# Strassen's seven products for the projections of an attention block, over four heads, on one Trainium2 core

## The chip, the cores and the metric

The kernel runs on one core of one Trainium2 chip. The metric is device time in microseconds (us). Three timed runs of the kernel before gave 1202.74, 1202.82 and 1204.02 us, median 1202.82 us. All data are float32. The big matmuls are done as three single-pass matmuls on a split of each operand into a high part (`hi`, type fp32r) and a rest (`lo`): hi·hi + hi·lo + lo·hi. The helper `three` issues them, so lines L707 to L709 stand for nearly all of TensorE's work.

## The reference

Tokens: 2 batches of 512, hidden width 512. `xn = layernorm(x)`. Then

```
qkv  = silu(xn @ qkv_w.T)                  # 32 heads x (q, k, v) x 128
scan over blocks of 32 tokens per head:    # linear attention with per-head decay
    scores = (q k^T) * diag_decay;  out = scores v + (q*q_decay) kv
    kv     = kv*block_decay + (k*k_decay)^T v
attn = rmsnorm(all heads, over 4096) * norm_w
gate = sigmoid(xn @ gate_w.T)              # 4096 wide
y    = (gate * attn) @ out_w.T             # 4096 -> 512
ffn  = xn @ W_base.T + b + routed LoRA experts (top 2 of 8, rank 16)
out  = x + y + ffn
```

The projections (q, k, v, gate) are 1024 tokens x 512 x 16384 and are more than half of the arithmetic. The kernels replace the scan by the equal full form: for each head and batch, scores of 512 x 512 (lower blocks only), times a decay table, times v.

## The kernel before

`acc` holds x, later the sum of the output projection. The front normalises the tokens in two halves (batch 0 first), turns them with TensorE transposes and splits them into `xhi` and `xlo`. ScalarE meanwhile fills `decay`, the decay tables of all 32 heads (L355).

The main part is a loop over 16 groups of two heads; each group has four steps `s` (head `s // 2`, batch `s % 2`). A step on TensorE is: `project` q (4 slices of the hidden width x 3 matmuls of 128 x 512), `attend` of the step before, in the first two steps `project_v` (4 token tiles, 12 matmuls of 128 x 256 each), `project` k, `project` the gate, in two of the four steps `output` (4 tiles, 6 matmuls of 128 x 512 each), then `scores` of this step. Each engine has this order written out by hand in its own block; semaphores tie them. PSUM's eight banks are two for projections (`proj`), three for scores, one for `att`, two for output tiles (`outp`).

Around it: ScalarE reads a projection from PSUM into SBUF through Silu or Tanh (L409, L437, L447, L456), copies it to the `hi` part (L415, L441, L451), and splits weight chunks (L364). VectorE subtracts to get the `lo` part (L572, L580, L583), multiplies scores by the table (L597), splits them (L602), gates (L544, L549) and adds output tiles into `acc` (L555). GpSimd makes the `lo` part of the weights (L301, 128 x 512 each) and the sum of squares (L320). The SP queue loads weight chunks of 256 KB five slots ahead.

The tail (after the last group) does the router (L846), the last attention step, the top-2 routing as a chain of small VectorE operations (L640 to L678), the base and expert matmuls into all eight banks, and adds everything (L693, L697). The base matmul is 96 matmuls of 128 x 512.

Of the kernel before, what the change touches and what calls it, by code (L numbers as in the profile page):

```python
# [11 lines left out]
P = 128  # L26
# [5 lines left out]
GH = 2  # L32
GROUPS = HEADS // GH
STEPS = GH * BATCH
# [4 lines left out]

V_AT = (1, 1 + TB)  # L40
PROJ = 3 * STEPS + NTB
PROJ0 = (0, 3 + TB, 2 * (3 + TB), 2 * (3 + TB) + 3)


SPLIT = TB - 1
P_LEN = tuple(SEQ - P * j for j in range(TB))
P_AT = tuple(sum(P_LEN[:j]) for j in range(TB))
P_COLS = sum(P_LEN[:SPLIT])

ORDER = (3, 0, 1, 2)  # L50

FIRST_CHUNKS = 5
CONSTS = 5
RAW_SLOTS = 5
GROUP_CHUNKS = 10

# [9 lines left out]

def build(nc, x, w_chunks, norm_w, a_router, b_base, slopes, out):
    x_tok = x.rearrange("b (t p) c -> p (b t) c", p=P)  # L70
    out_tok = out.rearrange("b (t p) c -> p (b t) c", p=P)

    ctx = ExitStack()
    with ctx:
        def sb(name, shape, dt=F32):
            return ctx.enter_context(nc.sbuf_tensor(name, shape, dt))

        def bank(name):
            return ctx.enter_context(nc.psum_tensor(name, [P, 512], F32))
# [3 lines left out]


        xhi = sb("xhi", [P, KC, BATCH * SEQ], F32R)
        xlo = sb("xlo", [P, KC, BATCH * SEQ], F32R)

        acc = sb("acc", [P, NTB, HID])

        decay = sb("decay", [P, HEADS, 2 * P])  # L90
        table = sb("table", [P, SEQ])

        raw = sb("raw", [P, RAW_SLOTS, 512])
        qkg_hi = [sb(f"qkg_hi{i}", [P, 3, KC * P], F32R) for i in range(GH)]
        qkg_lo = [sb(f"qkg_lo{i}", [P, 3, KC * P], F32R) for i in range(GH)]
        wv_hi = sb("wv_hi", [P, 2, 512], F32R)
        wv_lo = sb("wv_lo", [P, 2, 512], F32R)
        wo_hi = sb("wo_hi", [P, GH, HID], F32R)
        wo_lo = sb("wo_lo", [P, GH, HID], F32R)

        qf = sb("qf", [P, SEQ])
        kf = sb("kf", [P, SEQ])
        q_hi = sb("q_hi", [P, SEQ], F32R)
        q_lo = sb("q_lo", [P, SEQ], F32R)
        k_hi = sb("k_hi", [P, SPLIT * P], F32R)
        k_lo = sb("k_lo", [P, SPLIT * P], F32R)
        vf = [sb(f"vf{i}", [P, GH * D]) for i in range(SPLIT)]
        v_hi = [sb(f"v_hi{b}", [P, SPLIT, GH * D], F32R) for b in range(BATCH)]
        v_lo = [sb(f"v_lo{b}", [P, SPLIT, GH * D], F32R) for b in range(BATCH)]
        v_last = [sb(f"v_last{b}", [P, GH * D]) for b in range(BATCH)]  # L110
        pf = sb("pf", [P, sum(P_LEN)])
        p_hi = sb("p_hi", [P, P_COLS], F32R)
        p_lo = sb("p_lo", [P, P_COLS], F32R)
        tanh_g = sb("tanh_g", [P, SEQ])
        square = sb("square", [P, SEQ])
        gated = sb("gated", [P, SEQ])
        g_hi = [sb(f"g_hi{s}", [P, SEQ], F32R) for s in range(STEPS)]
        g_lo = [sb(f"g_lo{s}", [P, SEQ], F32R) for s in range(STEPS)]
        sum_sq = sb("sum_sq", [P, BATCH, SEQ])

# [5 lines left out]
        half_norm = sb("half_norm", [P, HEADS])  # L126
        minus_half = sb("minus_half", [P, NTB])
# [5 lines left out]
        diff = square[:, 0:2 * P]  # L133

        free = decay[:, :, :].rearrange("p h n -> p (h n)")
        taken = [0]

        def take(*shape):
            n = 1
            for d in shape:  # L140
                n *= d
            part = free[:, taken[0]:taken[0] + n]
            taken[0] += n
            if len(shape) == 1:
                return part
            names = "abc"[:len(shape)]
            sizes = {k: d for k, d in zip(names, shape)}
            return part.rearrange(f"p ({' '.join(names)}) -> p {' '.join(names)}", **sizes)

        x_again = take(NTB, HID)  # L150
        ar = take(KC, ER + EXPERTS)
        base_b = take(HID)
        h_keep = take(NTB, ER)
        sm = [take(NTB, EXPERTS) for _ in range(8)]
        sm1 = [take(NTB) for _ in range(8)]
        xf = [qf, kf, pf[:, 0:HID], pf[:, HID:2 * HID]]
        hw_hi = g_hi[0:2]
        hw_lo = g_lo[0:2]

        proj = [bank(f"proj{i}") for i in range(2)]  # L160
        score = [bank(f"score{i}") for i in range(3)]
        att = bank("att")
        outp = [bank(f"outp{i}") for i in range(2)]
        S = {j: score[i % 3][:, 0:P_LEN[j]] for i, j in enumerate(ORDER)}

        turn = [score[0], score[1], att, outp[0]]
        ffn = [proj[0], proj[1], score[2], outp[0], outp[1], att, score[0], score[1]]


        x_in = [sem(f"x_in{t}") for t in range(NTB)]  # L170
        slope_in = sem("slope_in")
        raw_in = [sem(f"raw_in{i}") for i in range(RAW_SLOTS)]
        norm_in = sem("norm_in")
        again_in = sem("again_in")
        consts = sem("consts")
        diff_made = sem("diff_made")
        decay_made = sem("decay_made")
        ln = sem("ln")
        pow_ready = sem("pow_ready")
        pow_done = sem("pow_done")  # L180
        xn_ready = sem("xn_ready")
        turned = sem("turned")
        xhi_done = sem("xhi_done")
        xlo_done = sem("xlo_done")
        acc_zero = sem("acc_zero")
        whi_done = sem("whi_done")
        wlo_done = sem("wlo_done")
        proj_ready = sem("proj_ready")
        proj_free = sem("proj_free")
        qhi_done = sem("qhi_done")  # L190
        qlo_done = sem("qlo_done")
        khi_done = sem("khi_done")
        klo_done = sem("klo_done")
        vhi_done = sem("vhi_done")
        vlo_done = sem("vlo_done")
        gate_done = sem("gate_done")
        table_done = sem("table_done")
        scores_ready = sem("scores_ready")
        masked = sem("masked")
        phi_done = sem("phi_done")  # L200
        plo_done = sem("plo_done")
        att_ready = sem("att_ready")
        gated_done = sem("gated_done")
        ghi_done = sem("ghi_done")
        glo_done = sem("glo_done")
        square_done = sem("square_done")
        summed = sem("summed")
        out_ready = sem("out_ready")
        acc_done = sem("acc_done")
        late_in = sem("late_in")  # L210
        xf_done = sem("xf_done")
        h_ready = sem("h_ready")
        h_read = sem("h_read")
        route = sem("route")
        route_act = sem("route_act")
        rms_ready = sem("rms_ready")
        hw_done = sem("hw_done")
        hw_turned = sem("hw_turned")
        hwhi_done = sem("hwhi_done")
        hwlo_done = sem("hwlo_done")  # L220
        xb_done = sem("xb_done")
        part_done = sem("part_done")
        ffn_ready = sem("ffn_ready")
        result_done = sem("result_done")
        stored = sem("stored")

# [694 lines left out]
```

## Time and profile before

| quantity | value |
|---|---|
| time, median of three | 1202.82 us |
| profiled execution: span | 1201.3 us |
| profiled execution: its own time | not given apart from the span; the median lies 1.5 us above the span |
| TensorE (PE) busy | 1170.9 us, 97% of the span |
| VectorE (DVE) busy | 716.2 us, 60% |
| ScalarE (ACT) busy | 523.2 us, 44% |
| GpSimd (POOL) busy | 343.4 us, 29% |
| granted TensorE clock | 1.000 of full speed |

PE's busy time counts matmuls that overlap in the pipeline, so a row's duration (0.39 us for 128 x 512) is longer than the step from one matmul to the next; that step is the useful price, and is read as the distance between start times. PEld is the weight load, which runs beside the matmuls. For the other engines, a duration includes an end that overlaps the next instruction of the same engine when that one waits for nothing.

### The profile page before, as it was taken

The numbers are of one execution on the slowest core, as the hardware profiler recorded it, in microseconds if no ns is written. First come the engines' busy times: TensorE is split into PE (matmuls) and PEld (weight loads), VectorE is DVE, ScalarE is ACT, GpSimd is POOL, SyncE is SP. The second block draws the span as 40 slices with busy tenths as digits, with TensorE's granted clock in tenths as the row PEclk, the third lists the DMA queues.
The fourth block names the chain that finished last, engine by engine and source line by source line (L and its number), as shares of the span: only waits on it lengthen the run. The fifth ranks groups of instructions, "written<-read, shape, count | busy, mean of one in ns | idle before, by whom it ended". The sixth has DMA issues, their size and how long they took to land.

```text
span 1201.3 us, 18952 instructions
## 1 busy us (share of the span) xinstructions
PE 1170.9 (97%) x6256; PEld 1013.1 (84%) x6256; DVE 716.2 (60%) x1216; ACT 523.2 (44%) x1076; POOL 343.4 (29%) x253
## 2 busy tenths in 40 slices
PE   5999999999999999999999999999999999999998
PEld 4888888888888888888888888888888888888887
DVE  6664655656565664655556465655656556465667
ACT  7543535434453543445344343543445354344520
POOL 3332313313231331323223131331323133132323
PEclk9999999999999999999999999999999999999999
DMA  4121101101011110201101010110111111020301
GB/s 159 36 53 36 53 18 44 44 17 52 27 43 35 33 54 18 52 17 44 44 22 54 29 52 17 44 44 17 52 35 40 30 36 51 17 52 25 106 1 70
DMA packets 27694, 50.31 MB, mean 42 GB/s; under 512 B 3232, under 2 KB 3232, under 8 KB 27680
## 3 DMA queue, kind: packets, MB, share of 16 engines
q1 hardware_dynamic: 27392, 50.10, 14.2%
q8 instruction: 8, 0.13, 0.0%
q10 hardware_dynamic: 288, 0.03, 0.0%
q14 instruction: 6, 0.05, 0.0%
HBM read 48.02 MB, written 2.10 MB: 42 GB/s over the span
## 4 chain that ended last, share of the span: by engine, by line
PE 83%; ACT 6%; DVE 5%; issue 5%; DMA 0%; ACTq 0%; POOL 0%; DVEq 0%; SPq 0%; POOLq 0%
PE proj L707 17%; PE proj L709 16%; PE proj L708 16%; PE outp L707 5%; PE outp L709 5%; PE outp L708 5%; PE score L709 3%; PE score L708 3%; PE score L707 3%; PE att L707 2%; PE att L709 2%; PE att L708 2%; DVE k_lo L583 2%; DVE gated L544 2%; PE score L779 2%
## 5 line engine op out<-in xcount | busy, mean ns | idle before, releaser
L707 PE MATMUL proj<-xhi,qkg_hi 128*128 128x512 f32 x768 | 303.5, 395 | 1.5 <-DVE xlo L525 1.5
L709 PE MATMUL proj<-xhi,qkg_lo 128*128 128x512 f32 x768 | 299.7, 390 | 0.0
L708 PE MATMUL proj<-xlo,qkg_hi 128*128 128x512 f32 x768 | 299.7, 390 | 0.0
L301 POOL TENSOR_TENSOR qkg_lo<-raw,qkg_hi 128x512 fp32r<-128x512 f32 x99 | 128.0, 1294 | 565.6 <-ACT qkg_hi L364 565.6
L462 ACT ACTIVATE p_hi<-pf 128x512 fp32r<-128x512 f32 (+2 forms) x192 | 86.6, 515 | 247.0 <-DVE pf L597 247.0
L709 PEld LDWEIGHTS proj<-xhi,qkg_lo 128*128 128x128 f32 x768 | 144.1, 188 | 31.5
L707 PEld LDWEIGHTS proj<-xhi,qkg_hi 128*128 128x128 f32 x768 | 144.4, 188 | 27.7 <-DVE xlo L525 1.8
L708 PEld LDWEIGHTS proj<-xlo,qkg_hi 128*128 128x128 f32 x768 | 144.5, 188 | 26.0
L555 DVE TENSOR_TENSOR acc<-acc,outp 128x512 f32<-128x512 f32 x128 | 88.1, 688 | 116.0 <-PE outp L709 116.0
L707 PE MATMUL proj<-wv_hi,xhi 128*128 128x256 f32 (+1 forms) x514 | 151.0, 294 | 4.1 <-ACT vf L437 2.6
L572 DVE TENSOR_TENSOR q_lo<-qf,q_hi 128x512 fp32r<-128x512 f32 x64 | 86.7, 1354 | 112.7 <-ACT q_hi L415 112.7
L709 PE MATMUL proj<-wv_hi,xlo 128*128 128x256 f32 (+1 forms) x514 | 145.4, 283 | 0.0
L708 PE MATMUL proj<-wv_lo,xhi 128*128 128x256 f32 (+1 forms) x514 | 145.4, 283 | 0.0
L597 DVE TENSOR_TENSOR pf<-score,table 128x128 f32<-128x128 f32 (+3 forms) x256 | 113.7, 486 | 43.4 <-PE score L779 33.9
L549 DVE TENSOR_TENSOR g_lo<-gated,g_hi 128x512 fp32r<-128x512 f32 x64 | 104.7, 1636 | 46.0 <-ACT g_hi L427 45.3
L583 DVE TENSOR_TENSOR k_lo<-kf,k_hi 128x384 fp32r<-128x384 f32 x64 | 65.9, 1029 | 90.3 <-ACT k_hi L451 88.2
L320 POOL TENSOR_TENSOR sum_sq<-sum_sq,square 128x512 f32<-128x512 f32 x64 | 109.0, 1704 | 24.1 <-ACT square L471 22.7
L707 PEld LDWEIGHTS proj<-wv_hi,xhi 128*128 128x128 f32 x514 | 98.1, 191 | 10.5 <-ACT vf L437 10.4
L301 POOL TENSOR_TENSOR wo_lo<-raw,wo_hi 128x512 fp32r<-128x512 f32 x32 | 41.2, 1286 | 219.8 <-ACT wo_hi L364 219.8
L707 PE MATMUL outp<-wo_hi,g_hi 128*128 128x512 f32 x256 | 99.7, 389 | 1.1 <-DVE g_lo L549 1.1
L708 PE MATMUL outp<-wo_lo,g_hi 128*128 128x512 f32 x256 | 99.6, 389 | 0.0
L709 PE MATMUL outp<-wo_hi,g_lo 128*128 128x512 f32 x256 | 99.6, 389 | 0.0
(193 smaller groups left out, 1978.2 us busy)
## 6 DMA issues: line engine op xcount, KB each, us to landing
raw<-w_chunks SPq DMA_DIRECT2D x165, 256.0 KB, 2.6
acc<-x SPq DMA_DIRECT2D x8, 256.0 KB, 5.9
decay<-x SPq DMA_DIRECT2D x1, 2048.0 KB, 10.6
out<-acc SPq DMA_DIRECT2D x8, 256.0 KB, 2.0
decay<-a_router SPq DMA_DIRECT2D x1, 272.0 KB, 3.0
decay<-b_base SPq DMA_DIRECT2D x1, 256.0 KB, 5.1
slope<-slopes ACTq DMA_DIRECT2D x1, 16.0 KB, 5.0
norm<-norm_w ACTq DMA_DIRECT2D x1, 16.0 KB, 5.5
```

The source lines that it names most:

```text
L301: pool.tensor_tensor(lo, raw[:, slot, :], hi.bitcast(F32), ALU.subtract).then_inc(wlo_done, 1)
L320: pool.tensor_tensor(sum_sq[:, b, :], sum_sq[:, b, :], square[:], ALU.add).then_inc(summed, 1)
L462: act.activation(p_hi[:, cols], pf[:, cols], ACT.Copy).then_inc(phi_done, 1)
L544: dve.tensor_tensor(gated[:], att[:, :], tanh_g[:], ALU.mult).then_inc(gated_done, 1)
L549: dve.tensor_tensor(g_lo[s][:], gated[:], g_hi[s][:].bitcast(F32), ALU.subtract).then_inc(glo_done, 1)
L555: dve.tensor_tensor(acc[:, b * TB + t, :], acc[:, b * TB + t, :], outp[t % 2][:, :], ALU.add).then_inc(acc_done, 1)
L572: dve.tensor_tensor(q_lo[:], qf[:], q_hi[:].bitcast(F32), ALU.subtract).then_inc(qlo_done, 1)
L583: dve.tensor_tensor(k_lo[:], kf[:, 0:SPLIT * P], k_hi[:].bitcast(F32), ALU.subtract).then_inc(klo_done, 1)
L597: dve.tensor_tensor(pf[:, P_AT[j]:P_AT[j] + P_LEN[j]], S[j], table[:, 0:P_LEN[j]], ALU.mult).then_inc(masked, 1)
L707: pe.matmul(out_, a_hi, b_hi, start=start, stop=False)
L708: pe.matmul(out_, a_hi, b_lo, start=False, stop=False)
L709: return pe.matmul(out_, a_lo, b_hi, start=False, stop=stop)
```

## The change

All of `build` is rewritten. What it does:

**Products.** Tokens of the two batches and the two halves of the hidden width form a 2 x 2 block matrix (t). Two heads' columns (or two heads' q and k) form the other (w). A *unit* computes all four blocks of the product, 128 x 512 each times two, by seven products instead of eight (Strassen in Winograd's form). A product is 2 slices x 3 = 6 matmuls of 128 x 512, or 12 of 128 x 256 where tokens are the stationary side (units V1, V2 and the base matmul). The seven token operands `t_hi`, `t_lo` are made once in the front. The weight operands are made for each unit: GpSimd makes four combinations of 128 x 256 (`combine`), ScalarE copies seven blocks of 256 to `w_hi` (`weight`), GpSimd subtracts for `w_lo` (`low`).

**Putting the products together** takes three PSUM banks p, q, r and one SBUF tile x (`xs`): per unit ScalarE copies three results to SBUF (`copy_m1`, `copy_u2`, `copy_u3`) and VectorE adds three times (`make_u2`, `make_c22`, `make_c12`), each 128 x 512. TensorE may start product 7 only after `copy_u2`, product 4 after `copy_u3`, product 3 after `make_c22`. Products 1, 6 and 5 open the banks p, q and r anew and wait until the unit before has been drained from them (`free`).

**Loops.** The main loop has 8 bodies (first, 6 in a hardware loop, last) of four heads: units V1, V2 (v of four heads), QK1, QK2, QK3 and QK0 (q and k of a head, QK0 for the next body), G23, G01 (gates). In the last body QK0 and G01 are the base matmul. Two units (QK0, G01 of the first body) come ahead of the loop.

**Operands stay in PSUM.** Silu is applied in place in the bank; the table is multiplied in place in the score bank; gating is done in place in `att`. So the `lo` subtractions read one operand from PSUM, except for the tile x. `outp` has one bank instead of two.

**Front and tail.** The router and the top-2 routing move to the front, with the eight tiles normalised together; the decay tables go to DRAM (`near_dram`, 4 MB written) and come back one head at a time; the x + bias term goes through DRAM too. The tail keeps four output tiles, the expert matmuls and the sums.

Core of the diff, TensorE's side:

```diff
+            def product(g, i, m, by_token=False):
+                n = unit(g, i)
+                b = BANK_OF[m]
+                if m in (1, 5, 6):
+                    at_least(pe, free[b], n)
+                else:
+                    pe.wait_ge({7: u2_copied, 2: m1_copied, 4: u3_copied, 3: c22_made}[m], n + 1)
...
+                pe.wait_ge(wlo[PIECE_OF[m]], n + (2 if by_token and pair == 0 else 1))
...
+                    for kc in range(2):
+                        w = slice(kc * P, kc * P + P)
+                        mm = three(banks[b], w_hi[i % 2][:, wi, w], w_lo[i % 2][:, wi, w], t_hi[:, ti, kc, :], t_lo[:, ti, kc, :],
+                                   fresh and kc == 0, kc == 1)
...
+                output(-4)
+                scores(0)
+                output(-3)
+                prod(V1, 1, 6)
+                output(-2)
+                prod(V1, 5, 7, 2, 4, 3)
+                prod(V2, 1, 6)
+                output(-1)
+                prod(V2, 5, 7, 2, 4, 3)
+                attend(0)
+                scores(1)
+                prod(QK1, 1, 6, 5, 7, 2)
+                attend(1)
+                prod(QK1, 4, 3)
+                prod(QK2, 1, 6, 5)
+                scores(2)
+                prod(QK2, 7, 2, 4, 3)
+                attend(2)
+                scores(3)
+                prod(G23, 1, 6)
+                output(0)
+                prod(G23, 5)
+                output(1)
...
+                prod(G01, 2)
+                output(11)
+                attend(7)
+                prod(G01, 4, 3)
```

VectorE's and ScalarE's orders at four places (VectorE after V1 and after QK1, ScalarE in QK1 and at the end of a body):

```diff
+                make_c22(V1)
+                lo(V1, "p")
+                make_c12(V1)
+                lo(V1, "x")
+                lo(V1, "q")
+                lo(V1, "r")
+                make_u2(V2)
...
+                make_c12(QK1)
+                lo(QK1, "q")
+                gated_lo(1)
+                make_u2(QK2)
+                lo(QK1, "r")
...
+                probs01(1)
+                copy_m1(QK1)
+                gated_hi(0)
+                probs2(1)
+                out_weight(0)
+                copy_u2(QK1)
...
+                gate(G01, "p")
+                squares(7)
+                gate(G01, "q")
+                gated_hi(7)
```

The front on VectorE (`routing` is the chain of small operations) and on ScalarE:

```diff
+            make_u2(LAST + G01)
+            make_far(0)
+            make_c22(LAST + G01)
+            make_c12(LAST + G01)
+            routing()
+            dve.wait_ge(near_made, HEADS + 2)
...
+            weight(V1, 1)
+            weight(V1, 2)
+            silu(LAST + QK0, "p")
```

## Rows read from the trace of the kernel before

**Rows 1.** The page's first part: busy time of each engine, share, instructions.

```profile
PE 1170.9 (97%) x6256; PEld 1013.1 (84%) x6256; DVE 716.2 (60%) x1216; ACT 523.2 (44%) x1076; POOL 343.4 (29%) x253
```

**Rows 2.** TensorE's waits: engine and line that waited, for whom, us in total, times, longest.

```profile
PE score L716 <- DVE acc L519: 13.2, 1, 13.2
```

**Rows 3.** Three stretches (front, one group, tail): length, busy and instructions per engine, clock.

```profile
0.00:18.00 18.00, 3.29 (x16) 3.08 (x16) 9.84 (x22) 12.51 (x33) 5.49 (x15) 1.00 0.58 206
...
520.00:591.20 71.20, 70.49 (x378) 61.02 (x378) 41.72 (x69) 31.34 (x64) 19.84 (x14) 1.00 0.12 37
...
1156.00:1201.30 45.30, 40.97 (x224) 34.82 (x222) 31.94 (x88) 3.97 (x6) 13.35 (x10) 0.99 0.13 47
```

**Rows 4.** Timeline, TensorE: start us, duration us, line, operation; pairs that give a distance.

```profile
500.20 0.39 PE L707 MATMUL proj<-xhi,qkg_hi 128*128 128x512 f32 x1
...
500.88 0.39 PE L707 MATMUL proj<-xhi,qkg_hi 128*128 128x512 f32 x1
...
509.04 0.38 PE L779 MATMUL score<-qf,kf 128*128 128x128 f32 x2
...
510.85 0.39 PE L707 MATMUL proj<-xhi,qkg_hi 128*128 128x512 f32 x1
...
513.61 0.39 PE L707 MATMUL att<-p_hi,v_hi 128*128 128x512 f32 x1
...
515.33 0.36 PE L707 MATMUL proj<-wv_hi,xhi 128*128 128x256 f32 x1
...
515.76 0.28 PE L707 MATMUL proj<-wv_hi,xhi 128*128 128x256 f32 x1
...
516.12 0.28 PE L707 MATMUL proj<-wv_hi,xhi 128*128 128x256 f32 x1
```

**Rows 5.** Timeline, VectorE's table of a group's first head, in groups 1 and 7.

```profile
86.54 0.48 DVE L568 TENSOR_SCALAR table<-decay,far 128x128 f32 x2
...
513.57 0.48 DVE L568 TENSOR_SCALAR table<-decay,far 128x128 f32 x2
```

**Rows 6.** Groups by line and shape: busy us, mean ns, idle before.

```profile
L555 DVE TENSOR_TENSOR acc<-acc,outp 128x512 f32<-128x512 f32 x128 | 88.1, 688 | 116.0 <-PE outp L709 116.0
...
L572 DVE TENSOR_TENSOR q_lo<-qf,q_hi 128x512 fp32r<-128x512 f32 x64 | 86.7, 1354 | 112.7 <-ACT q_hi L415 112.7
...
L409 ACT ACTIVATE qf<-proj 128x512 f32<-128x512 f32 x64 | 38.3, 599 | 103.0 <-PE proj L709 103.0
...
L364 ACT ACTIVATE qkg_hi<-raw 128x512 fp32r<-128x512 f32 x98 | 60.9, 623 | 0.0
...
L301 POOL TENSOR_TENSOR qkg_lo<-raw,qkg_hi 128x512 fp32r<-128x512 f32 x99 | 128.0, 1294 | 565.6 <-ACT qkg_hi L364 565.6
```

**Rows 7.** Timeline of handovers: who starts how long after whom.

```profile
499.04 1.74 POOL L320 TENSOR_TENSOR sum_sq<-sum_sq,square 128x512 f32<-128x512 f32 x1
...
499.55 0.68 DVE L544 TENSOR_TENSOR gated<-att,tanh_g 128x512 f32<-128x512 f32 x1
...
500.65 0.39 PE L709 MATMUL proj<-xhi,qkg_lo 128*128 128x512 f32 x1
...
501.08 0.60 ACT L447 ACTIVATE kf<-proj 128x512 f32<-128x512 f32 x1 [0.18 <-PE proj L709]
...
1111.37 0.39 PE L707 MATMUL proj<-wv_hi,xhi 128*128 128x256 f32 x1 [0.18 <-ACT vf L437]
```

**Rows 8.** Timeline: runs on ScalarE and VectorE, part of the routing chain, the last sum.

```profile
2.96 8.07 ACT L355 ACTIVATE decay<-square 128x256 f32<-128x256 f32 x26
...
17.88 2.46 DVE L505 BATCH_NORM_STATS2 stats<-acc 128x6 f32<-128x512 f32 x4
...
1176.51 0.21 DVE L658 TENSOR_REDUCE decay<-decay 128x8 f32<-128x64 f32 x1
...
1182.32 1.71 DVE L678 TENSOR_TENSOR decay<-decay 128x128 f32<-128x128 f32 x8
...
1198.15 0.69 DVE L693 TENSOR_TENSOR acc<-score,acc 128x512 f32<-128x512 f32 x1 [1.77 <-PE score L709]
```

More of the change, by code:

```diff
@@ L150, in build @@
[L150 to L163, printed above, removed]
@@ new lines, in _ @@
+            whole(LAST + QK0, "p")
+            silu(LAST + QK0, "q")
+            hi(LAST + QK0, "p")
+            whole(LAST + QK0, "q")
+            weight(V1, 4)
+            hi(LAST + QK0, "q")
+            silu(LAST + QK0, "r")
+            weight(V1, 3)
+            whole(LAST + QK0, "r")
+            whole(LAST + QK0, "x")
+            hi(LAST + QK0, "r")
+            hi(LAST + QK0, "x")
+            weight(V2, 1)
+            copy_m1(LAST + G01)
+            copy_u2(LAST + G01)
+            copy_u3(LAST + G01)
@@ L477, in _ @@
+            weight(V2, 2)
+            gate(LAST + G01, "p")
+            gate(LAST + G01, "q")
+            gate(LAST + G01, "x")
+            weight(V2, 3)
             for t in range(2):
                 act.wait_ge(hw_turned, t + 1)
-                act.activation(hw_hi[t][:], score[t][:, :], ACT.Copy).then_inc(hwhi_done, 1)
+                copy(hw_t[:, 512 * t:512 * t + 512], score[:, t, :]).then_inc(hwt_done, 1)
+            act.wait_ge(near_out, 64)
+            body(0, first=True)
+            with act.Fori(1, SGS - 1) as g:
+                body(g)
@@ new lines, in _ @@
+            make_u2, make_c22, make_c12, lo = units(0)
+            for t in range(NTB):
+                dve.wait_ge(x_in[t], 16)
+                dve.bn_stats(stats[:, t, :], acc[:, t, :]).then_inc(ln, 1)
+            done[0] += NTB
+            dve.wait_ge(ln, done[0])
+            for t in range(NTB):
+                dve.bn_aggr(mean_var[:, t, :], stats[:, t, :]).then_inc(ln, 1)
+            done[0] += NTB
+            dve.wait_ge(ln, done[0])
+            dve.tensor_scalar(rs[:, 0, :], mean_var[:, :, 1], EPS, None, ALU.add).then_inc(pow_ready, 1)
@@ L869, in _ @@
-            base(5)
-            pe.wait_ge(hwlo_done, 2)
-            for t in range(NTB):
-                if t >= 6:
-                    base(t)
-                expert(t)
+            pe.wait_ge(hwt_done, 2)
+            body(0, first=True)
+            with pe.Fori(1, SGS - 1) as g:
+                body(g)
+            body(SGS - 1, final=True)
 def kernel(L0_attn_hidden_states, L0_attn_qkv_w, L0_attn_out_w, L0_attn_gate_w, L0_attn_norm_w,
```

1769 lines of the change are left out of this document (1173 added, 596 removed).

## The prediction

> **What bounds the kernel now.** I read the busy shares first: TensorE has work in 97% of the span, no other engine more than 60% [rows 1]. Next, its waits: the only long one is the 13.2 us before its first transpose [rows 2]. Then the stretches: a front of 18.0 us in which TensorE does 3.3 us, groups in which it is busy 70.5 of 71.2 us, a tail of 45.3 us; the granted clock is 1.00 to 0.99, its upper level of 2.4 GHz, throughout [rows 3]. So TensorE's own steps set the time, and a change is worth what it takes off them plus what it does to the front, the tail and the waits.
>
> The timeline gives the steps. Three matmuls of 128x512 take 500.88 - 500.20 = 0.68 us, 0.2275 each; three of 128x256 take 0.36 us, 0.120 each; one `scores` takes 510.85 - 509.04 = 1.81 us, one `attend` 515.33 - 513.61 = 1.72 us [rows 4]. A group has 144 projection matmuls (32.8 us), 96 of 256 for v (11.5), 48 for output tiles (10.9) and 4 x 3.53 (14.1): 69.3 us. The group's real period is (513.57 - 86.54)/6 = 71.17 us [rows 5], so 1.9 us of a group are waits. Four heads cost 142.3 us now.
>
> **TensorE's steps after the change.** A unit has 7 x 6 = 42 matmuls of 512 instead of 48: 9.56 us; by token 84 of 256, 10.1 us. A body: six units 57.3, two by token 20.2, 16 output tiles x 6 x 0.2275 = 21.8, eight scores and attends 28.2: 127.5 us, against 138.6 for two groups' steps. The first body lacks four output tiles (-5.5), the last has two units by token (+1.1). Eight bodies: 1020 - 5.5 + 1.1 = 1015.6 us.
>
> **Do the other engines have room?** Prices: VectorE 0.69 us for 128x512 with a PSUM operand, ScalarE 0.60 to 0.62, GpSimd 1.29 [rows 6]; 26 ScalarE instructions of 256 in a row take 8.07 us, 0.31 each [rows 8], from which 512 in a row is about 0.52 and each has 0.1 fixed. ScalarE in a body: 166 instructions over 73,700 columns (24 product copies, 44 Silu and whole parts, 24 high parts, 34 weight copies and so on); at 0.83 ns a column and 0.1 each, 61 + 17 = 78 us. VectorE: 137 instructions over 59,400 columns, at 1.05 ns and 0.15 each 62 + 21 = 83 us. GpSimd: 74 instructions over 28,700 columns; at 1.29/512 a column 72 us, with sums of squares at 1.74 [rows 7] 76 us. Its combinations of 256 columns have no row: half of 1.29 at least, 1.29 at most, by which the 76 could be 107; I take the lower, as the bulk is columns. An instruction that also writes PSUM in place has no row either; the nearest reads PSUM at 0.69, and I take that; from 0.1 less to 0.2 more for some 60 of them moves VectorE to 77 to 95 us. All stay below 127.5, so none is a bound by its sum. What remains is where TensorE waits for a short chain.
>
> The `lo` subtractions change in kind. `q_lo`, with two SBUF operands, takes 1.35 us [rows 6], while `gated`, which reads PSUM, took 0.68 inside a GpSimd instruction (499.04 to 500.78) [rows 7]. After the change all but those of tile x read PSUM; I price them at 0.69 and tile x at 0.69 to 1.35.
>
> **Waits inside a body.** Handover prices: the consumer starts 0.03 to 0.04 us after the producer's row ends (500.65 + 0.39, then 501.08; I take the same between the others), a matmul's row ends 0.16 after the next could start (0.39 - 0.2275), so a reader starts 0.2 us after TensorE has gone on; a restart costs 0.1 (0.39 against 0.28 at 1111.37) [rows 7]. A product is 1.365 us.
>
> - Product 7 needs product 6, `make_u2`, `copy_u2`: 0.2 + 0.69 + 0.03 + 0.60 + 0.04 = 1.56 us, with product 5 (1.365) above it. In seven units an output tile or `scores` stands between as well. In QK1 nothing does, and ScalarE has `gated_hi(0)`, `probs2(1)` and `out_weight(0)` (1024 columns, 0.95) ahead of `copy_u2`, whose chunk is asked for only when QK1's weights are split. I work out 0.5 to 1.6; I take 0.8 us.
> - V1 to V2: product 6 of V2 needs bank q drained. ScalarE is done with q in time, but VectorE's order has `make_c12` (product 3's end + 0.2 + 0.69), then `lo` of x (0.69 to 1.35), then `lo` of q (0.69). From product 3's end this is 2.3 to 2.9 us, against 1.44 for product 1 of V2: 0.9 to 1.5; I take 1.2.
> - QK1 to QK2: `lo(QK1,"q")` ends 1.5 us after product 3, against 1.365: 0.25 with the restart. Then the real one: VectorE does `make_u2(QK2)` before `lo(QK1,"r")`. So product 5 of QK2, which opens r, waits for product 6's end + 0.2 + 0.69, then 0.56 for 384 columns, + 0.1: 1.55 us.
> - End of a body: `output(-4)` needs attend(7)'s squares, gating, `gated_hi`, `gated_lo`: 0.8, 1.5, then ScalarE first does `gate(G01,"q")`, which waits for product 4 (to 2.2), then 2.8, 3.5 us, against 2.73 for products 4 and 3: 0.9 with the restart.
> - Products 4 and 3 have 0.5 and 1.2 us to spare over `copy_u3` and `make_c22`; QK3 and QK0 have an attend ahead of the next unit; weights come 2 us or more ahead. I take nothing for them.
>
> Sum 4.8 us a body, 38 in all. Bodies: 1054 us, a period of 132.3 against 142.3.
>
> **The front grows.** Eight tiles are normalised together: four tiles' statistics take 2.46 us [rows 8], so eight, the last load among them, end near 11 us (an estimate); with power, refinement and eight tiles through TensorE and ScalarE (0.52 each, beside two splits) they are turned by 22. Token operands are nine passes of 1024 columns on VectorE (1.2 each), two SBUF operands each, beside three of 2.6 on GpSimd; by the `q_lo` row a meeting costs 0.66; a pass that meets one of these might wait 2.6. I allow 3 us in all, from 1 to 8. Product 1 starts near 20, but products 5, 6, 7, 4 wait one by one for their operands; the first unit ends at 38. ScalarE meanwhile does twelve tables (12 x 0.31), a table load, then G01's weights; it then stands in `weight(V1,2)` until GpSimd has made G01's lower parts (4.6) and V1's combinations (3), to 50, before it drains the first unit's banks. So G01 runs from 53 to 64. `routing()` stands behind `make_c12` on VectorE: from L658 on it takes 1182.32 + 1.71 - 1176.51 = 7.5 us [rows 8], some 2 more before that. With two copies the first `scores` starts at 76 us; from 64 on nothing hides the 12 us. Now the first projection starts at 18.0 [rows 3]. 76, from 68 to 86.
>
> The Trainium skill, "SBUF — State Buffer", section "Who interferes with whom", says that a VectorE instruction with two SBUF inputs and a GpSimd instruction that reads SBUF exclude each other, the later one blocked until the other's end. By it three meetings would cost up to 7.8 us instead of the 3, the front would be 81 and the sum 1163; the `q_lo` and `gated` rows agree with it.
>
> **The tail shrinks.** After the last product VectorE does `make_c12` and base sums (0.69 each, to 3.7), two experts, refinement (6.4), then four output tiles through one bank: each 1.365 + 0.2 + 0.69, to 14.0; six expert sums, eight results (0.66 each) and a refinement, 24.4; the last store lies 1201.3 - 1198.84 = 2.5 us behind the last sum [rows 3, 8]: 27 us, from 24 to 31, where now the stretch is 45.3, which holds the base matmul.
>
> **Sum.** 76 + 1054 + 27 = 1157 us of span; the median lies 1.5 above the span of the profiled execution: 1158.5. Against 1201.3: front +58, groups 1139 to 1054, tail -18.
>
> **Rivals.**
> - *Waits small.* If the orders interlock better than my worst readings (2 us a body, not 4.8) and the front is 70: 1130 us. For it: the present orders leave only 1.9 us a group [rows 5]. Against it: the `make_u2` before `lo` of r is in the code. 0.15.
> - *ScalarE late at the copies (the other side).* ScalarE works in order, and each unit needs it at `copy_u2` and `copy_u3` within 0.5 us. If at seven units a body a weight copy (0.3 to 0.95 us) that waits for GpSimd or a chunk stands in front, each costs about 1.2 us beyond my sum, 8.4 a body: 1158 + 67 = 1225 us. It decides from 5.6 us a body beyond the 4.8, where 1203 is reached. For it: GpSimd's 76 us may be 107, and it holds ScalarE at every second and fourth weight piece. Against: weights stand two units ahead, and sums leave 40% free. 0.12.
> - *Half of that*, 1170 to 1203: 2 to 5 us a body more than I found. 0.23.
> - *The clock falls.* In short stops between matmuls, or in the 12 us stop, the granted clock could go to 1.2 GHz, where steps double; 5% of the bodies at that level would cost 50 us: 1208. The row of the front shows 1.00 with TensorE idle for 15 of 18 us [rows 3]. The Trainium skill, "TensorE: Matmul & The Clock Gate", section "A second HAM failure mode: psum-queue depth-cycling", says small idle times between groups of matmuls can make the clock go up and down; the trace of before does not show it. 0.03.
> - *It does not save the products.* The count of matmuls in the code is plain: below 0.01.
>
> **How the numbers follow.** My forecast's case (1138 to 1175) has 0.47, predicted 1158. The range of 8 in 10 takes the small-waits case and nearly all of the half case: 1125 to 1203. Below 0.2% (2.4 us) a measurement of this kernel can't tell a change from none. Slower than 1205: the late copies, part of the clock case: 0.12. Within: 0.02. Faster: 0.86.
>
> **What would show it.** TensorE's count near 5,900 instead of 6256, in steps of 0.2275 us; a body period of 132 us; the longest repeated wait at product 5 of QK2 for `lo` of r, then product 6 of V2, the tile at the body's start and product 7 of QK1; the first `scores` at 76 us after a stop of some 12; tail 27 us; `lo` at 0.69 us from PSUM. I am wrong if the period is above 138, if GpSimd's busy share is above 80%, or if TensorE waits at `copy_u2` or `copy_u3` in most units.

## The result: slower, with the profile after

The changed kernel takes 1243.2 us (median of 4 runs, 1241.9 to 1244.1) against 1202.8: a ratio of 1.033, 95% interval 1.032 to 1.034. Forecast were 1158.5 us, 1125 to 1203. The profiled execution has a span of 1241.8 us, 1.4 below the median. Two of the kernels below had one run each far outside all others (3259 and 2571 us), which their medians and ranges leave out.

First the page of the kernel after: busy times as in [rows 1], then the span in 40 slices, TensorE's busy tenths and its granted clock.

```profile
PE 1118.3 (90%) x5848; PEld 956.0 (77%) x5848; DVE 689.5 (56%) x1212; ACT 679.7 (55%) x1401; POOL 641.2 (52%) x629
...
PE   3477989989999899989999899989999899989995
...
PEclk9779899999999899989999899989999899989999
```

The reader is to see two things. TensorE has 408 matmuls fewer, as it should, and is busy 90% of the span, no longer 97%. Single slices, again and again, show 8 instead of 9, in the busy row and in the clock row alike: something in each body stops TensorE, and behind it the clock is lower.

TensorE's waits, as in [rows 2]: for whom, us in total, times, longest.

```profile
PE bank_q L1350 <- ACT ys L531: 40.0, 9, 7.1
PE score L1528 <- DVE acc L1260: 20.3, 1, 20.3
PE bank_p L1350 <- DVE q_lo L979: 14.2, 1, 14.2
PE bank_r L1350 <- DVE q_lo L979: 11.0, 8, 1.4
PE score L1552 <- DVE h_keep L1327: 6.7, 1, 6.7
PE outp L1350 <- DVE g_lo L1052: 5.9, 7, 0.9
...
PE bank_q L1350 <- DVE v_lo L979: 4.4, 8, 0.5
```

The four waits that the forecast had named are the four that repeat in the bodies, and three are its size or smaller. `ys` is what `copy_u2` writes: the wait of product 7 of QK1, forecast at 0.8 us, is eight of the nine waits and 35.2 of the 40.0; it is 3.8 to 4.4 us in bodies 2 to 8 and 7.1 in the first, which has the ninth, of 4.8, too.

The stretches, with columns as in [rows 3]: the front up to the first `scores`, the loop's bodies from 240 to 1080, one body from product 6 of V2 to the same in the next, 8.2 us of that body, and the tail.

```profile
0.00:85.15 85.15, 39.58 (x189) 32.77 (x189) 44.27 (x88) 43.54 (x94) 43.45 (x46) 0.85 0.35 120
...
240.00:1080.00 840.00, 798.52 (x4161) 682.73 (x4160) 470.95 (x823) 483.79 (x997) 447.64 (x444) 0.98 0.13 41
...
529.99:669.80 139.81, 133.00 (x692) 113.68 (x693) 78.35 (x137) 80.54 (x168) 74.62 (x74) 0.98 0.13 41
551.80:560.00 8.20, 8.11 (x27) 6.65 (x28) 1.38 (x3) 4.26 (x11) 5.71 (x4) 0.66 0.24 78
...
1213.40:1241.80 28.40, 15.30 (x66) 11.08 (x64) 18.09 (x36) 0.00 (x0) 2.49 (x2) 0.91 0.20 74
```

Against the forecast's span of 1157:

| part | forecast us | measured us |
|---|---|---|
| front, to the first `scores` | 76 | 85.15 |
| eight bodies | 1054 | 1128.25 |
| of them a steady body's period | 132.3 | 139.8 |
| tail | 27 | 28.4 |
| span | 1157 | 1241.8 |

Of the 84.8 us missing, 74 lie in the bodies: 7.5 for each of eight, and 14 more: some 13 in the first body, the rest in the last.

Now one of these stops in the timeline (start, duration, engine, line, and in brackets how long the engine was idle before and whom it waited for).

```profile
542.28 1.29 POOL L391 TENSOR_TENSOR w_lo<-raw,w_hi 128x512 fp32r<-128x512 f32 x1 [3.05 <-ACT w_hi L531]
...
545.69 0.28 DVE L1027 TENSOR_TENSOR p_end<-score,table 128x128 f32<-128x128 f32 x1
...
546.30 0.33 SPq L263 DMA_DIRECT2D table<-near_dram  x1
...
546.90 0.86 SPq L249 DMA_DIRECT2D raw<-w_chunks  x2
...
550.29 1.06 ACT L531 ACTIVATE wo_hi<-raw 128x1024 fp32r<-128x1024 f32 x1 [3.56 <-DMA raw<-w_chunks]
...
551.26 0.58 ACT L531 ACTIVATE ys<-bank_q 128x512 f32<-128x512 f32 x1
...
551.89 0.79 PE L1350 MATMUL bank_q<-t_hi,w_hi 128*128 128x512 f32 x1 [3.93 <-ACT ys L531]
...
552.48 0.63 PE L1351 MATMUL bank_q<-t_lo,w_hi 128*128 128x512 f32 x1
```

Read from the end. Product 7 waits 3.93 us for `copy_u2` (`ys`). `copy_u2` stands behind `out_weight(0)` (`wo_hi`), for whose chunk ScalarE was idle 3.56 us. GpSimd had done with that chunk's buffer at 543.57. But SyncE issued the load only at 546.90: ahead of it in its queue is `load_near(4 * g + 1)`, the next head's tables, which waits until VectorE has used the tables that stand in its place (L1027, 545.69). So 3.3 us passed in SyncE's queue. And the matmuls behind the stop last 0.79 and 0.63 us in steps of 0.43, where 0.39 and 0.2275 are usual: the granted clock is 0.66 in the mean of the 8.2 us, so in most of them it is 0.5, the lower level of 1.2 GHz.

Against a body without this stop (first experiment below) the period is 5.6 us longer. The stop has 3.1 of them (3.93 against 0.86). The other 2.5 are what is left, and the slow matmuls make up nearly all of it: 12 matmuls in steps of 0.43 in place of 0.2275 are 2.4 us.

### The profile page after: what moved, and what is told of

Its sections match the earlier page's. It is cut to its first block, busy times and chain, and to the rows that moved or that the text cites. A ratio compares the mean times of both kernels' runs of the same rounds, so it can differ in the third digit from the quotient of the medians.

```text
span 1241.8 us, 18953 instructions
## 1 busy us (share of the span) xinstructions
PE 1118.3 (90%) x5848; PEld 956.0 (77%) x5848; DVE 689.5 (56%) x1212; ACT 679.7 (55%) x1401; POOL 641.2 (52%) x629
## 4 chain that ended last, share of the span: by engine, by line
PE 78%; DVE 9%; issue 4%; DMA 3%; ACT 3%; POOL 1%; SPq 1%; DVEq 0%; ACTq 0%; POOLq 0%
PE bank_q L1350 8%; PE bank_q L1352 7%; PE bank_q L1351 7%; PE outp L1350 5%; PE outp L1352 4%; PE outp L1351 4%; PE bank_p L1351 4%; PE bank_p L1350 4%; PE bank_p L1352 4%; PE bank_r L1350 4%; PE bank_r L1352 4%; PE bank_r L1351 4%; PE att L1350 3%; PE att L1352 3%; PE att L1351 3%
## 5 line engine op out<-in xcount | busy, mean ns | idle before, releaser
L391 POOL TENSOR_TENSOR w_lo<-combo,w_hi 128x768 fp32r<-128x768 f32 (+1 forms) x132 | 170.1, 1291 | 206.5 <-ACT w_hi L531 206.2
L391 POOL TENSOR_TENSOR w_lo<-raw,w_hi 128x256 fp32r<-128x256 f32 (+1 forms) x132 | 135.6, 1032 | 172.0 <-ACT w_hi L531 171.8
L1350 PE MATMUL bank_q<-t_hi,w_hi 128*128 128x512 f32 x288 | 121.9, 423 | 43.7 <-ACT ys L531 40.0
L1352 PE MATMUL bank_q<-t_hi,w_lo 128*128 128x512 f32 x288 | 118.1, 410 | 0.0
L1351 PE MATMUL bank_q<-t_lo,w_hi 128*128 128x512 f32 x288 | 117.8, 409 | 0.0
L531 ACT ACTIVATE p_hi<-score 128x896 fp32r<-128x896 f32 (+1 forms) x128 | 81.2, 653 | 62.5 <-DVE score L1020 62.3
L1350 PE MATMUL outp<-wo_hi,g_hi 128*128 128x512 f32 x256 | 103.0, 403 | 12.2 <-DVE g_lo L1052 5.9
L1350 PEld LDWEIGHTS bank_q<-t_hi,w_hi 128*128 128x128 f32 x288 | 56.6, 197 | 61.6 <-ACT ys L531 43.8
L1350 PE MATMUL bank_p<-t_hi,w_hi 128*128 128x512 f32 x192 | 79.9, 416 | 14.2 <-DVE q_lo L979 14.2
L1350 PE MATMUL bank_r<-t_hi,w_hi 128*128 128x512 f32 x192 | 76.1, 396 | 11.0 <-DVE q_lo L979 11.0
L531 ACT ACTIVATE w_hi<-combo 128x768 fp32r<-128x768 f32 (+1 forms) x132 | 81.2, 628 | 8.7 <-POOL combo L384 6.8
L1351 PE MATMUL bank_p<-t_lo,w_hi 128*128 128x512 f32 x192 | 79.6, 415 | 0.0
L1352 PE MATMUL bank_p<-t_hi,w_lo 128*128 128x512 f32 x192 | 79.3, 413 | 0.0
```

The costliest lines, as they stand in the source:

```text
L391: pool.tensor_tensor(piece(w_lo[i % 2], j), piece_source(i, j), piece(w_hi[i % 2], j).bitcast(F32), ALU.subtract).then_inc(wlo[j], 1)
L531: return act.activation(out_, in_, ACT.Copy, **kw)
L1350: pe.matmul(out_, a_hi, b_hi, start=start, stop=False, skip_group_check=True)
L1351: pe.matmul(out_, a_hi, b_lo, start=False, stop=False, skip_group_check=True)
L1352: return pe.matmul(out_, a_lo, b_hi, start=False, stop=stop, skip_group_check=True)
```

## The experiments

Theory after the comparison: (A) the late chunk in SyncE's queue delays `copy_u2`, and the stop brings the lower clock with it. Rivals: (B) ScalarE's order alone, whatever the chunk; (C) the clock falls by the kernel's many short stops, not by this one. All times are medians, ratios are to the kernel before, run on the same chip.

**SyncE's order alone.** In a body the chunk for `out_weight(0)` is asked for ahead of the tables:

```diff
-                load_near(4 * g + 1)
                 unit_taken(g, QK1)
                 load_rows(0, 20 * g + 8, 20 * g + 9)
+                load_near(4 * g + 1)
```

> SP's order: the load of the output weights' chunk (asked for when QK1's weights are split) goes ahead of the load of the decay table of head 1, which waits in the same queue until step 1's scores are masked. ScalarE's order unchanged. Theory A': the chunk is late because of that wait in SP's queue: it is issued 3.2 us earlier (right after GpSimd's 543.57 instead of 546.90), product 7's wait falls from 3.9 to about 1.0 us, the clock stays up, 1197 us. Theory D (the chunk is late because of its transfer, or GpSimd): no change, 1240 or more.

Measured: 1203.4 us (1200.8 to 1209.7, 10 runs), ratio 1.0006 (0.9991 to 1.0021): 39.8 us less than the changed kernel. Its timeline around product 7, then the six bodies from 240 to 1080:

```profile
532.38 0.94 SPq L249 DMA_DIRECT2D raw<-w_chunks  x2
534.79 0.33 SPq L263 DMA_DIRECT2D table<-near_dram  x1
...
535.84 1.06 ACT L531 ACTIVATE wo_hi<-raw 128x1024 fp32r<-128x1024 f32 x1 [0.49 <-DMA raw<-w_chunks]
...
536.80 0.58 ACT L531 ACTIVATE ys<-bank_q 128x512 f32<-128x512 f32 x1
...
537.43 0.50 PE L1350 MATMUL bank_q<-t_hi,w_hi 128*128 128x512 f32 x1 [0.86 <-ACT ys L531]
...
240.00:1080.00 840.00, 817.18 (x4378) 702.29 (x4377) 504.08 (x854) 505.95 (x1045) 464.41 (x458) 1.00 0.13 42
```

The load now goes 2.4 us ahead of the tables, `ys` is in time, product 7 waits 0.86 us (0.43 to 0.94 over bodies 2 to 8), which is the 0.8 of the forecast, and the loop's clock is 1.00. The period is 134.2 us. The time is 6 us above the expected 1197: the first body takes 147.0 us where it took 147.3, since stops of 3.60, 2.35, 3.31 and 4.78 us stand there in place of 7.10 and 4.79. (C) falls here: with stops of 0.43 to 1.38 us in every body the clock does not move. The forecast had cited a rule beside its clock rival (the Trainium skill, "TensorE: Matmul & The Clock Gate", section "A second HAM failure mode: psum-queue depth-cycling": small idle times between groups of matmuls can make the clock go up and down): for these stops the trace does not agree. One exchange of two lines in a queue that does no arithmetic was worth nearly half of the miss.

**ScalarE's order alone.** `copy_u2(QK1)` and `copy_u3(QK1)` ahead of `out_weight(0)` and two weight pieces; SyncE as in the changed kernel:

```diff
-                out_weight(0)
                 copy_u2(QK1)
+                copy_u3(QK1)
+                out_weight(0)
                 weight(QK2, 2)
                 weight(QK2, 4)
-                copy_u3(QK1)
```

> ScalarE's order in QK1: copy_u2 and copy_u3 ahead of out_weight(0) and QK2's weight copies. Theory A (product 7 of QK1 waits only because copy_u2 stands in ScalarE's queue behind out_weight(0), whose chunk lands late, and the stop lets the clock fall to its lower level, which costs 2.6 us more a body): the 3.9 us wait goes to 0.4, the granted clock stays 1.00 from the second body on, the period falls from 139.8 to about 133.7, the time from 1243 to about 1191 us. Theory B (the low clock comes from the body's load, not from the stop): the wait goes but the stretches at half clock stay, about 1215 us. Theory C (the wait only moves, to QK2's weights): above 1230 us.

Measured: 1232.5 us (1230.6 to 1234.6), 1.0245 (1.0228 to 1.0263). Product 7's wait in QK1 is gone, and another grew: `PE bank_r L1350 <- DVE q_lo L979`, product 5 of QK2, 23.2 us in 8 waits where it had been 11.0. Of a body's 139.8 us only 1.7 were won. The time is that of the third theory, though the wait moved to another place than it said. (B), ScalarE's order alone, does not explain the loss.

**Both together**, the two edits above in one kernel.

> Both edits (copies first, chunk first). Theory A and A': product 7's wait 0.3 to 0.4, nothing behind it late, clock 1.00 in the loop: 133.5 us a body, about 1188 us; at most 4 us better than copies first alone. If GpSimd's lower parts were the next to be late, the chunk's earlier load would help more, 1180.

Measured: 1232.0 us (1229.6 to 1234.0), 1.0238 (1.0219 to 1.0256), no better than ScalarE's order alone and 29 us worse than SyncE's. A miss, and the most useful one. Its timeline, then its six bodies:

```profile
408.75 0.60 ACT L531 ACTIVATE xs<-bank_q 128x512 f32<-128x512 f32 x1 [1.75 <-PE bank_q L1352]
409.24 1.05 ACT L531 ACTIVATE wo_hi<-raw 128x1024 fp32r<-128x1024 f32 x1
...
416.31 8.69 SPq L249 DMA_DIRECT2D raw<-w_chunks  x5
...
419.61 0.42 ACT L531 ACTIVATE w_hi<-raw 128x256 fp32r<-128x256 f32 x1 [2.12 <-DMA raw<-w_chunks]
...
419.93 0.58 ACT L531 ACTIVATE q_hi<-bank_r 128x512 fp32r<-128x512 f32 x1
...
421.29 0.52 PE L1350 MATMUL bank_r<-t_hi,w_hi 128*128 128x512 f32 x1 [2.90 <-DVE q_lo L979]
...
422.03 0.63 PE L1352 MATMUL bank_r<-t_hi,w_lo 128*128 128x512 f32 x1
...
240.00:1080.00 840.00, 807.07 (x4243) 691.62 (x4242) 479.81 (x830) 489.58 (x1009) 448.46 (x444) 0.98 0.13 41
```

`out_weight(0)` (`wo_hi`) came later on ScalarE, now behind `copy_u3` (`xs`), which waits for product 7 itself. So its lower part came later on GpSimd, so the buffer came free later and the next chunks were loaded later; ScalarE then stood 2.12 us in `weight(G23, 1)`, which is ahead of `hi(QK1, "r")` in its order. A copy moved forward had put a wait for a transfer in front of another copy. (That `copy_u3` is the one is shown below, by the kernel that moves `copy_u2` alone.) The lower clock came back too (0.63 us matmuls, 0.98).

**Keep the stop, by another cause.** `copy_u2` first as above, but TensorE waits for `out_weight(0)` before product 7 of QK1:

```diff
-                prod(QK1, 1, 6, 5, 7, 2)
+                prod(QK1, 1, 6, 5)
+                pe.wait_ge(wohi, 2 * g + 1)
+                prod(QK1, 7, 2)
```

> copy_u2 ahead of out_weight(0) on ScalarE, but TensorE itself waits, before product 7 of QK1, until out_weight(0) is done: the same stop of about 3.8 us, held by a wait of TensorE's own. Theory A: the stop alone makes both losses, so the time stays at 1240 to 1246 us with the same half-clock stretch of 6.8 us in each body. Theory B or any in which ScalarE's lateness has other victims: clearly below, 1215 to 1230 us.

Measured: 1233.7 us (1232.0 to 1238.2), 1.0243 (1.0222 to 1.0263), period 139.0, 31.4 us in 8 waits there. This lies between the two expectations. Against the kernel with SyncE's order mended, the stop alone keeps 4.8 of the 5.6 us a body, with ScalarE free to run on; it is also a little shorter, and shrinks from 3.83 us in body 2 to 3.20 in body 8. These are the 8 us behind it in bodies 4, 5 and 8, after stops of 3.64, 3.40 and 3.20 us:

```profile
552.00:560.00 8.00, 8.00 (x26) 6.53 (x27) 1.27 (x2) 4.06 (x10) 6.08 (x4) 0.62 0.18 46
691.60:699.60 8.00, 8.00 (x32) 6.72 (x33) 2.35 (x4) 4.71 (x11) 6.85 (x5) 0.81 0.15 47
1106.01:1114.01 8.00, 8.00 (x38) 6.79 (x39) 3.35 (x5) 6.03 (x14) 7.73 (x5) 1.00 0.19 52
```

The granted clock is 0.62, 0.81 and 1.00: in this place the longer stop has more slow matmuls behind it, and that of 3.20 us has none.

**A stop of another length**, on the kernel with SyncE's order mended: TensorE waits for VectorE's second table before product 7.

```diff
+                pe.wait_ge(tab_made, 8 * g + 4)
```

> Base: chunk first (1203.4 us). Added: TensorE waits before product 7 of QK1 until VectorE has made head 1's far tables, a stop of some 1.5 to 2.5 us in each body where it was 0.65, and nothing else is held. Theory A (a stop of 3.9 us brings the clock down, a short one does not): the granted clock stays 1.00 in the loop, the time grows by the longer stop alone, 1 to 2 us a body: 1211 to 1219 us. Theory B (any added stop costs clock as well): half-clock stretches in the loop, 1230 us or more.

Measured: 1218.5 us (1216.5 to 1219.5), 1.013 (1.011 to 1.015), period 136.5, at the upper end of the first theory. Its product 7 and its six bodies:

```profile
404.48 0.50 PE L1350 MATMUL bank_q<-t_hi,w_hi 128*128 128x512 f32 x1 [3.13 <-DVE table L986]
...
240.00:1080.00 840.00, 803.44 (x4307) 690.67 (x4307) 491.86 (x839) 496.77 (x1027) 453.11 (x449) 1.00 0.13 41
```

The stop of 3.13 us costs 2.3 us a body more than the one of 0.7 in the mean that it replaces, and nothing else: the clock stays at 1.00. So stops are paid at least once, and the changed kernel's 3.93 us stop, and the 2.90 us one above, are paid a second time in slow matmuls. At product 7 of QK1, in bodies 2 to 8, the cases part by length: no slow matmul behind the eight stops of 3.12 to 3.20 us in this kernel and the one that keeps the stop; in that one 6 to 8 behind those of 3.31 to 3.46; and 7 to 13 behind those of 3.59 to 4.36, there and in the changed kernel. Across places they do not: at product 5 of QK2, in the two kernels with both copies first, all stops of 2.77 to 3.08 us have 6 to 13 slow matmuls behind them; TensorE had worked only 1.7 us between each and another stop of 0.7 to 1.0. And with SyncE's order alone, a stop of 3.60 us in the first body has none. What decides besides the length, these runs do not settle.

**The waits that the forecast had named.** Two more kernels, on top of SyncE's order. One puts `copy_u2(QK1)` ahead of `out_weight(0)` only, `copy_u3` where it was:

```diff
-                out_weight(0)
                 copy_u2(QK1)
+                out_weight(0)
```

> Base: chunk first. Added: only copy_u2(QK1) ahead of out_weight(0); copy_u3 keeps its place behind the weight copies. The wait of product 7 falls from 0.65 to 0.2 us, product 5 of QK2 unchanged: 1199 to 1201 us. If any delay of out_weight(0) makes GpSimd late and G23's chunk with it (what both edits together showed), product 5 of QK2 waits longer and the time is 1208 or more.

Measured: 1199.7 us (1198.2 to 1201.3), 0.9966 (0.9953 to 0.9978), period 133.7, as expected. This kernel differs from the one of both edits (1232.0 us) only in the place of `copy_u3`: `wo_hi` starts 0.15 us ahead of product 7 here and 2.19 us behind it there, and the wait of product 5 of QK2 is 1.38 us here and 2.90 there. So it was `copy_u3` that must not stand ahead of `out_weight(0)`.

The other lets bank r be drained first, on both engines:

```diff
+                lo(QK1, "r")
                 make_u2(QK2)
-                lo(QK1, "r")
...
-                copy_m1(QK2)
                 whole(QK1, "r")
-                weight(G23, 1)
                 hi(QK1, "r")
+                copy_m1(QK2)
+                weight(G23, 1)
```

> Base: chunk first. Added: VectorE makes the lower part of r (QK1) ahead of make_u2(QK2), and ScalarE makes its high part ahead of copy_m1(QK2) and G23's first weight copy. The forecast's third term: product 5 of QK2 waits 1.38 us now and 0.1 then, 1.3 us a body: 1193 us. If make_u2, now later, holds product 7 of QK2 instead: 1200 or more.

Measured: 1195.0 us (1191.0 to 1195.4), 0.992 (0.990 to 0.994), period 132.9. The wait of product 5 of QK2 is gone from the list: 1.3 us a body for the stop that the forecast had at 1.55.

**All orders together**: the three above, `lo` of q before `lo` of x behind V1, `gated_hi(7)` before `gate(G01, "q")`, in the front the first unit's copies ahead of V1's weights, and `weight(QK0, 1)` behind `copy_u2(G23)`. The last of these, as an example:

```diff
-                weight(QK0, 1)
                 copy_m1(G23)
                 copy_u2(G23)
+                weight(QK0, 1)
```

> Chunk first, u2 first, lo r first, and three more: lo of q ahead of lo of x after V1; gated_hi(7) ahead of the gate of q; in the front, the first unit's Silu and high parts ahead of V1's weight copies; QK0's first weight copy behind copy_u2(G23). Per body 0.4 + 1.3 + 0.5 + 0.8 = 3.0 us off 134.0; front 6 us earlier; first body's stop of 4.8 us gone: 1203 - 24 - 6 - 5 = 1168 us. If GpSimd's chain is the next bound, above 1180.

Measured: 1177.5 us (1175.3 to 1180.1), 0.978 (0.976 to 0.980), period 131.4; the first `scores` comes at 79.3. That is 9.5 us above the expected 1168, though the period fell by 2.8 us of the expected 3.0 and the front by 5.7 of 6. What is left of stops in a body is 0.29 and 0.42 us. The first body still had three, of 3.60, 4.65 and 1.90 us.

**The routing earlier.** On top of it:

```diff
             make_c12(LAST + G01)
-            routing()
...
+            routing()
             lo(LAST + QK0, "p")
```

> All the reorderings of the run with everything together, and `routing()` moved on VectorE from behind the gates' combinations to ahead of `lo` of the front's first unit, where VectorE is idle. Theory (the front is set by the order in which the routing, the tables and the first `scores` follow one another): the first `scores` comes at 72 to 74 us in the place of 79.3, the rest of the kernel stays, and the time is near 1171 us. Rival (the front is set by the passes over the tokens, whose lengths grow where GpSimd and VectorE meet; the routing is hidden): the first `scores` stays at 79 and the time at 1177.5 us, or worse where the routing now stands in front of the first unit's `lo`.

Measured: 1177.9 us (1177.3 to 1179.5), 0.979 (0.978 to 0.981): nothing. The theory fell. TensorE's two marks in the front are

```profile
65.97 0.79 PE L1350 MATMUL bank_p<-t_hi,w_hi 128*128 128x512 f32 x1 [18.43 <-DVE q_lo L979]
...
80.07 0.50 PE L1350 MATMUL score<-q_hi,k_hi 128*128 128x512 f32 x1 [0.74 <-ACT acc L531]
```

against 56.87 and 79.30 before the move. The stop of 7.11 us at the router's transposes is gone, and the one at bank p has grown from 8.09 to 18.43: VectorE does the routing from 49 to 65, and `lo` of the first unit, which frees bank p, stands behind it. The chain of small operations is the bound in either place, and it is not the same length in both. In its old place it took 7.8 us (70.2 to 78.0), in the new one 16.0 (49.35 to 65.3), while GpSimd makes the lower parts and combinations of the weights. Its last eight multiplications, after the move and before it:

```profile
59.46 5.85 DVE L1327 TENSOR_TENSOR h_keep<-h_keep,sm 128x128 f32<-128x128 f32 x8
...
76.30 1.70 DVE L1327 TENSOR_TENSOR h_keep<-h_keep,sm 128x128 f32<-128x128 f32 x8
```

The move was expected to gain 5 to 7 us, and the chain is 8.2 us longer beside GpSimd's work, which is enough to undo it. No run tested this by itself.

**The bias trip out of the first body.** On top of this one, tokens plus bias go through the DRAM earlier: GpSimd's first addition in the front, the second behind `combine(QK1)`, SyncE's store and reload ahead of its wait for the head's tables.

```diff
+            sp.wait_ge(xb_done, 1)
+            sp.dma_start(xb_dram[:, 0:TB, :], acc[:, TB:, :]).then_inc(xb_out, 16)
+            sp.wait_ge(xb_out, 16)
+            sp.dma_start(acc[:, TB:, :], x_tok[:, TB:, :]).then_inc(xb_in[1], 16)
             sp.wait_ge(hwt_done, 2)
...
             low(V2, 2)
+            add_bias(0)
...
                 combine(QK1)
+                if first:
+                    add_bias(1)
...
-                    if first and s in (0, 2):
-                        add_bias(s // 2)
```

> As the run before it, and the trip of tokens plus bias through the DRAM moved out of the first body: GpSimd's first addition stands in the front behind the last `low`, its second in the first body behind the combination for QK1, and SyncE's store and reload ahead of its wait for the head's tables. Theory (the first body's three stops of 3.60, 4.65 and 1.90 us and the slow matmuls behind them come from this trip, in SyncE's queue and on GpSimd): most of them go, 8 to 12 us less than the run before it, near 1160 us if that gives 1171. Rival (the stops come from the first body's weights arriving late by themselves): the stops stay and the time moves by less than 3 us. Second rival (an addition of 4.6 us in the front blocks small copies of VectorE there): the first `scores` comes 2 to 4 us later and half of the gain goes.

Measured: 1160.7 us (1159.8 to 1161.2), 0.9643 (0.9627 to 0.9659): 17.2 us less, more than the theory's 8 to 12, and the fastest of all. In the run before it the first stop reads:

```profile
107.06 4.60 POOL L424 TENSOR_TENSOR acc<-acc 128x2048 f32<-128x2048 f32 x1
...
107.74 3.95 DVE L1042 COPY norm_now<-half_norm 128x4 f32<-128x4 f32 x1
...
112.32 0.69 ACT L531 ACTIVATE g_hi<-att,norm_now 128x512 fp32r<-128x512 f32 x1 [2.91 <-DVE att L1046]
...
114.45 0.60 ACT L531 ACTIVATE ys<-bank_q 128x512 f32<-128x512 f32 x1 [1.17 <-DVE bank_q L958]
...
115.10 0.63 PE L1350 MATMUL bank_q<-t_hi,w_hi 128*128 128x512 f32 x1 [3.60 <-ACT ys L531]
...
80.10:240.00 159.90, 147.10 (x778) 126.13 (x779) 86.97 (x145) 86.52 (x178) 87.36 (x82) 0.96 0.20 67
```

GpSimd adds the bias for 4.60 us. VectorE's copy of four numbers a partition, issued inside it, ends when GpSimd's addition does, 3.95 us later; the gating, `g_hi` and with it `ys` wait behind this copy. The Trainium skill, "SBUF — State Buffer", section "Who interferes with whom", says that a VectorE copy may take the ports it shares with GpSimd, and that then the one that comes second is blocked to the first one's end; the row agrees. Without the meeting (waits and the same 160 us of the last kernel):

```profile
PE bank_q L1350 <- ACT ys L531: 3.4, 9, 0.9
...
80.10:240.00 159.90, 157.05 (x894) 137.36 (x895) 92.84 (x159) 97.36 (x204) 91.46 (x87) 1.00 0.20 67
```

TensorE is busy 9.95 us more in the same stretch, at a clock of 1.00 in place of 0.96: stops of 3.60, 4.19 and 3.65 us had been there, and slow matmuls behind them. The first `scores` comes at 80.24 against 80.07, so the second rival falls as well. (The three stops went together; which part of the trip caused the second and the third was not separated.)

The whole way, each kernel on top of the one above it:

| kernel | us | period us |
|---|---|---|
| the changed kernel | 1243.2 | 139.8 |
| SyncE's order | 1203.4 | 134.2 |
| all orders | 1177.5 | 131.4 |
| bias trip early | 1160.7 | 131.4 |

## Why the prediction was wrong

**The step that failed** is the 0.8 us for product 7 of QK1. The forecast saw that `out_weight(0)` stands ahead of `copy_u2` and that its chunk is asked for late; it then took the middle of 0.5 to 1.6 without following that request through SyncE's queue, where it stands behind the next head's tables and VectorE's last use of the old ones. Measured 3.93 us, 3.1 more in a steady body. With SyncE's order mended the same term is 0.43 to 0.94, 0.7 in the mean.

**The clock was priced at nothing.** A rival had it, with 5% of the bodies at the lower level and a chance of 0.03. In fact the late copy and the lower clock come together: 2.5 us a body follow from the stop. They are one rival, not two: the stop, and the slow matmuls that follow it. The rival's share was near (some 5.5 of 139.8 us at the lower level, 4%), its price of 50 us too high (8 x 2.5 = 20), its chance far too low. No row of before could show this: [rows 3] shows 1.00 for a front in which TensorE had hardly begun to work, and within the groups its waits were 0.4 us at most:

```profile
PE score L779 <- DVE k_lo L583: 7.0, 16, 0.4
```

**The rest of the period.** The other waits measured 0.55 (forecast 1.2), 1.38 for the two at QK2 (1.8) and 0.86 (0.9): 1.1 us less. The last 3 us are time that the steps' sum leaves out, probably small gaps at each change of bank and of kind (they were not added up row by row): in the last kernel, with 0.3 and 0.43 us of stops, the period is still 131.4 against steps of 127.5. So 3.1 + 2.5 + 3.0 - 1.1 = 7.5. Two sums of the forecast were slightly off without changing it: its waits add up to 4.7 us, not 4.8, and GpSimd's 107 us need the 16 lower parts of 256 columns beside the 32 combinations, which alone give 97.

**The first body** lost some 13 us beyond this. The forecast had written its four missing output tiles as a gain and not looked at what it does in addition: two additions of 4.6 us on GpSimd, and a store that SyncE waits for between weight loads. That the last experiment gives back 17.2 shows the place. How the 13 splits between the blocked copy and the late chunks was not separated. In the last body 1.4 us are missing beyond the 7.5, which no run followed up.

**The front** was 9 us late. The small operations between the statistics and the first normalised tile ran to 19.6 (1.72 and 1.19 us for two of them, both inside a GpSimd subtraction), so the first transposes came at 20.3 and product 1 at 28.75, where the forecast had it near 20; the first unit ended at 48.9, not 38. The wait for the second unit (14.2 us) and the 22 us behind it are as forecast. Here are passes of the token operands:

```profile
28.66 3.42 POOL L492 TENSOR_TENSOR t_raw<-x_t 128x1024 f32<-128x1024 f32 x1 [9.09 <-ACT x_t L531]
...
29.88 3.29 DVE L1272 TENSOR_TENSOR t_raw<-x_t,t_raw 128x1024 f32<-128x1024 f32 x1
```

On GpSimd 3.42 us against the forecast's 2.6, on VectorE 3.29 against 1.2: they run at the same time and end within 1.1 us of each other. The forecast's other figure of 81 for the front, which counted full exclusion, is nearer to 85 than 76 was, but the miss began before the passes.

**What held.** The count (5848 for near 5,900), the step of 0.2275, `lo` from PSUM at 0.69 where [rows 6] has 1.35, combinations of 256 columns at 0.75 (near the lower of the two prices), the sums of the engines in a body (ScalarE 80.5 for 78, VectorE 78.4 for 83, GpSimd 74.6 for 76), the tail (28.4 for 27), and the order of the reading: no engine is the bound by its sum, the short chains are. The rival of ScalarE late at the copies had the right engine and side, but laid it on seven units a body at 1.2 us; it was one unit at 3.1, and behind ScalarE's wait stood SyncE's queue. The mended kernel takes 1160.7 us for a forecast of 1158.5; this is partly luck, since its front is 4 us longer than forecast and its period 0.9 us shorter, and it is another kernel than the one forecast.

## What to carry to other kernels

Where a copy stands behind a weight that comes by DMA, follow the load to its place in the queue that issues it, and name what that queue waits for first; a middle of two bounds is no price for it. Where TensorE never stops before a change and will stop for some microseconds after it, give the stop a second price, the slow matmuls behind it: here 2.5 us for a stop of 3.9, and nothing for those up to 1.38. Before a copy is moved forward, see what it waits for itself: everything behind it in the queue then waits for that too. And look at the first body of a loop by itself: what only it does is in no period.

## What was not expected of the hardware

- A VectorE copy of 128 x 4 elements took 3.95 us while GpSimd was inside an addition of 4.6 us. The table's multiplication (L986, 128 x 128, two) took 2.62 us in place of 0.47 beside GpSimd's `wo_lo` of 2.42: with the chunk in time the two meet, and 33.5 us in all replace 18.5 for that line.
- A stop of 3.93 us is followed by some 5.5 us at the lower clock, and one of 2.90 us in another kernel by slow matmuls too; one of 3.13 us in each body of a third kernel is followed by none. In one and the same place, stops of 3.64, 3.40 and 3.20 us are followed by 8 us at a mean clock of 0.62, 0.81 and 1.00.
- The same chain of small VectorE operations took 7.8 us, and 16.0 where GpSimd was at work beside it: eight multiplications of 128 x 128 took 5.85 us in place of 1.70.
- Moving a wait moved the loss but did not keep its size: the same edit of ScalarE's order was worth 10.7 us with SyncE's order as it was, and cost 28.6 with it mended.
